# Main maxima row and pattern maxima as four products in four row groups of TensorE

## What is computed

```python
qf = jnp.concatenate([q_nope, q_pe], -1)
kf = jnp.concatenate([k_nope, k_pe], -1)
scores = jnp.einsum('bhqd,bhkd->bhqk', qf, kf) * scale
probs = jax.nn.softmax(scores.astype(jnp.float32), axis=-1).astype(dt)
ctx = jnp.einsum('bhqk,bhkd->bhqd', probs, v)
main_out = ctx.transpose(0, 2, 1, 3).reshape(b, s, H * D_V) @ o_w.T

p_scores = jnp.einsum('bhqd,bhkd->bhqk', pq, pk) * PD ** (-0.5)
p_probs = jax.nn.softmax(p_scores.astype(jnp.float32), axis=-1).astype(dt)
p_ctx = jnp.einsum('bhqk,bhkd->bhqd', p_probs, pv)
pattern_out = p_ctx.transpose(0, 2, 1, 3).reshape(b, s, HID) @ sp_o_w.T
gates = jax.nn.softmax(hidden_states @ gate_w.T + gate_b, axis=-1)
return gates[..., 0:1] * main_out + gates[..., 1:2] * pattern_out
```

## Time and profile before

| | us |
|---|---|
| median of three runs | 800.05 (797.66 to 802.2) |
| profiled execution | 798.77 |
| its span, first to last instruction | 797.0 |

### The profile page before, as it was taken

One profiled execution on the slowest core, in us unless ns is written; L12 is line 12 of the kernel. 1 busy time (PEld: TensorE's weight loads), 2 busy tenths in 40 slices (PEclk: granted clock), 3 DMA queues, 4 the chain that ended last, 5 costly groups with the idle time before them and its releaser, 6 DMA issues. The chain is left out here.

```text
span 797.0 us, 13842 instructions
## 1 busy us (share of the span) xinstructions
PE 754.4 (95%) x5456; PEld 475.2 (60%) x5456; DVE 582.2 (73%) x673; ACT 392.9 (49%) x500; POOL 433.7 (54%) x277
## 2 busy tenths in 40 slices
PE   5888989999999999999999999999999999989995
PEld 5865655555656565656655556565656654438874
DVE  6857756766779677957776779677857799997647
ACT  4443445555555555554555555555555554542352
POOL 1243039554955495549545944594478446282433
PEclk9989999999999999999999999999999999999998
DMA  9796571016201630163026102620252413331001
GB/s 237 280 246 245 121 145 28 1 56 120 68 1 38 124 95 1 38 130 115 2 76 125 54 1 61 114 81 1 71 89 79 137 42 97 110 100 35 1 1 53
DMA packets 97796, 68.13 MB, mean 85 GB/s; under 512 B 66434, under 2 KB 76228, under 8 KB 97476
## 3 DMA queue, kind: packets, MB, share of 16 engines
q1 hardware_dynamic: 97732, 67.25, 33.3%
HBM read 41.23 MB, written 17.04 MB: 73 GB/s over the span
## 5 line engine op out<-in xcount | busy, mean ns | idle before, releaser
L1011 POOL TENSOR_TENSOR acc<-acc,em 128x1024 f32<-128x1024 f32 x96 | 237.2, 2471 | 55.1 <-ACT em L1068 52.2
L1148 DVE TENSOR_REDUCE m2p<-xb 128x2 f32<-128x1024 f32 x128 | 156.1, 1222 | 74.1 <-PE xb L1313 73.9
L1156 DVE TENSOR_REDUCE m<-xb 128x2 f32<-128x1024 f32 x128 | 155.9, 1218 | 53.9 <-PE xb L1313 53.8
L1059 ACT ACTIVATE ep<-xb 128x1024 f32<-128x1024 f32 x128 | 131.3, 1025 | 115.9 <-PE xb L1313 115.9
L1068 ACT ACTIVATE em<-xb 128x1024 f32<-128x1024 f32 x128 | 131.1, 1024 | 92.6 <-PE xb L1313 88.3
L1349 PE MATMUL pvm<-em,cpair 128*32 128x512 f32 x1024 | 136.7, 606 | 0.0
L974 POOL TENSOR_TENSOR rot<-rot,sin 128x512 f32<-128x512 f32 x32 | 41.2, 1287 | 126.7 <-DMA rot<-raw 126.7
L1313 PEld LDWEIGHTS xb<-pq,pk 49*128 49x128 f32 x256 | 23.9, 184 | 107.1 <-issue 99.5
L1011 POOL TENSOR_TENSOR acc<-em 128x1024 f32<-128x1024 f32 x16 | 38.2, 2387 | 76.1 <-PE xb L1462 67.1
L1360 PE MATMUL pvp<-ep,vp 128*32 128x512 f32 x512 | 66.7, 592 | 0.0
L1313 PE MATMUL xb<-pk,pq 48*128 48x512 f32 x256 | 56.6, 440 | 9.2 <-ACT ep L1059 4.7
(11 more groups left out here) (277 smaller groups left out, 1301.5 us busy)
## 6 DMA issues: line engine op xcount, KB each, us to landing
rot<-raw SPq DMA_DIRECT2D x128, 64.0 KB, 2.4
pk<-spqk_d SPq DMA_DIRECT2D x48, 128.0 KB, 4.2
sums<-rec_d SPq DMA_DIRECT2D x32, 128.0 KB, 2.8
ctx_d<-ctxr SPq DMA_DIRECT2D x14, 256.0 KB, 2.1
pq<-spqk_d SPq DMA_DIRECT2D x48, 64.0 KB, 2.3
wraw<-wst_d SPq DMA_DIRECT2D x7, 384.0 KB, 5.8
em<-in_o_w SPq DMA_DIRECT2D x1, 2048.0 KB, 7.6
vp<-vp_d SPq DMA_DIRECT2D x8, 256.0 KB, 4.5
```

Of the source, the lines that this page charges most:

```text
L1011: pool.tensor_tensor(acc[:, :, :], before, em[:, j:j + 2, :], ALU.add).then_inc(added, 1)
L1059: act.activation(ep[:, j:j + 2, :], src[:, :, :], ACT.Exp, scale=PAT_SCALE).then_inc(ep_ready, 1)
L1148: dve.tensor_reduce(m2p[:, 2 * tp:2 * tp + 2, t, kt], src[:, :, :], AX, ALU.max).then_inc(x_dve, 1)
L1156: dve.tensor_reduce(m2[:, q, :, t, kt], src[:, :, :], AX, ALU.max).then_inc(x_dve, 1)
```

## The change

In slots 1 to 7 (`quad_at`), in the steps that have pattern maxima, the step's main maxima `mm` come before `M`, and the first `pm` comes behind `M`. `M` leaves out its seventh pair; in its place, `quad` issues four products: `sel` with `mr` on 32 rows (0 to 31 and 64 to 95), which closes `M`, and the pattern maxima on 16 rows (32 to 47 and 96 to 111). A second `pm` of a step is one pair of 16 rows. The 16 rows are the third slot of the stacks, which now holds the high part of both queries and keys, so these maxima come from high x high alone. `load_stacks` only swaps which slot holds which part; its number of DMAs stays. Slot 0 keeps the 48-row products. `PM_STEP` becomes 1, 1, 1, 1, 2, 2, 1, 2, 1, 2, 1, 1 in steps 2 to 13, sixteen as before, so twelve quads a slot and 84 in all.

```diff
-PM_STEP = [0, 0, 1, 2, 1, 2, 1, 2, 1, 2, 1, 2, 1, 0, 0, 0]
+PM_STEP = [0, 0, 1, 1, 1, 1, 2, 2, 1, 2, 1, 2, 1, 1, 0, 0]
...
+def quad_at(v, s):
+    return 1 <= v < NP and PM_STEP[s] > 0
...
         if v <= NP:
             step.append(("T", s))
-        if v < NP:
-            step += [("pm", pm + i) for i in range(min(PM_STEP[s], 1))]
+        maxima = []
+        if v <= NP and s + MM_LATE < 16:
+            maxima.append(("mm", MM_LATE + s))
+        if v < NP and s >= 16 - MM_LATE:
+            maxima.append(("mm", s - (16 - MM_LATE)))
+        if quad_at(v, s):
+            step += maxima
         if v <= NP:
             step.append(("M", s))
-        if v < NP:
-            step += [("pm", pm + i) for i in range(1, PM_STEP[s])]
+        if quad_at(v, s):
+            step += [("pm", pm + i) for i in range(PM_STEP[s])]
             pm += PM_STEP[s]
-        if v <= NP and s + MM_LATE < 16:
-            step.append(("mm", MM_LATE + s))
-        if v < NP and s >= 16 - MM_LATE:
-            step.append(("mm", s - (16 - MM_LATE)))
+        else:
+            step += maxima
...
-                            lo = int(slot == (2 if w == 0 else 1))
+                            lo = int(slot == (0 if w else 1))
...
-                return paired(out, [(xkh, xqh), (xkh, xql), (xkl, xqh), (ykh, yqh), (ykh, yql), (ykl, yqh),
-                                    (sel[:, :], mr[:, queries])], 64)
+                pairs = [(xkh, xqh), (xkh, xql), (xkl, xqh), (ykh, yqh), (ykh, yql), (ykl, yqh)]
+                if quad_at(it + 1, s):
+                    return paired(out, pairs, 64, False)
+                return paired(out, pairs + [(sel[:, :], mr[:, queries])], 64)
+
+            def quad(v, s, i, out):
+                main, queries = x_bank(v, ("M", s)), half_of(s // NT)
+                for h in range(2):
+                    at = slice(64 * h, 64 * h + 32)
+                    mm = pe.matmul(main[:, h, :], sel[at, :], mr[at, queries], start=False, stop=True)
+                mm.then_inc(x_ready, 1)
+                return pattern_maxima(v, i, out)
+
+            def pattern_maxima(v, i, out):
+                b, t, tp, kt = v % 2, i // 4, i // 2 % 2, i % 2
+                for h in range(2):
+                    at = slice(64 * h + 2 * PD, 64 * h + 3 * PD)
+                    mm = pe.matmul(out[:, h, :], pq[at, b, tp, t::4], pk[at, b, tp, half_of(kt)], start=True, stop=True)
+                return mm
```

More of the change, by code:

```diff
@@ L1306, in passes, with paired @@
                 return mm
-            def paired(out, pairs, rows):
+            def paired(out, pairs, rows, closed=True):
                 for n, (w, x) in enumerate(pairs):
@@ L1312, in paired @@
                         at = slice(64 * h, 64 * h + rows)
-                        mm = pe.matmul(out[:, h, :], w[at, :], x[at, :], start=(n == 0), stop=(n == len(pairs) - 1))
+                        mm = pe.matmul(out[:, h, :], w[at, :], x[at, :], start=(n == 0),
+                                       stop=(closed and n == len(pairs) - 1))
                 return mm
@@ L1362, in pattern_values, with x_tile @@
                 mm.then_inc(pvp_done, 1)
-            def x_tile(v, tile):
+            def x_tile(v, s, tile):
                 kind, i = tile
@@ L1376, in x_tile @@
                     mm = main_scores(v - 1, i, out)
+                    if quad_at(v, s):
+                        return
                 elif kind == "P":
@@ L1409, in x_tile @@
                     t, tp, kt = i // 4, i // 2 % 2, i % 2
-                    mm = paired(out, [(pq[:, b, tp, t::4], pk[:, b, tp, half_of(kt)])], 3 * PD)
+                    if v == 0:
+                        mm = paired(out, [(pq[:, b, tp, t::4], pk[:, b, tp, half_of(kt)])], 3 * PD)
+                    elif x_tiles[n - 1][1][0] == "M":
+                        mm = quad(v, s, i, out)
+                    else:
+                        mm = pattern_maxima(v, i, out)
                 elif kind == "mm":
@@ L1467, in tensor_program @@
                     for tile in xs[v][s]:
-                        x_tile(v, tile)
+                        x_tile(v, s, tile)
                     if s == 0 and v >= 2:
```

## The result

The kernel after takes 804.71 us (median of 12 runs, 801.82 to 806.76) against 799.62 us for the kernel before beside it (12 runs, 796.91 to 802.2): a ratio of 1.0071 [1.0055, 1.0087], slower by 5.1 us. The profiled execution took 803.35 us, 801.6 of them span, 4.6 more than before.

A forecast was written before the change was run, and what follows sets the result against it. TensorE was taken as the bound from step 6 to the next slot's step 1; steps 2 to 5 gain 0.71 us, later steps lose 2.23, +10.4 us over seven slots, giving 810 us, range 787 to 818.

The forecast's parts named there:

- the sum: Over slots 1 to 7: +1.52 us in each of six slots and +1.27 in slot 7, +10.4 us.
- What bounds the kernel: TensorE's work is on the path from step 6 to the next slot's step 1; steps 3 to 5 have waits.
- The price of the quad: Each quad costs 0.09 + 0.46 = 0.55 us against 0.47 for the pairs removed: +0.08 where TensorE is the path.
- Rival (a): In each quad, 32-row groups mix with 64-row products for free, 0.31 us cheaper: 790 us; chance 0.22.
- Rival (b): The quad's four products don't run side by side or their loads queue, 0.23 us more: 829 us; chance 0.12 with smaller form.
- Rival (c): The switch is paid, but the quad's strided loads cost no more than plain ones, 0.42 us: 799 us; chance 0.10.
- The wait after steps 4, 8 and 12: The next step's `mm` waits for the buffer of `M`, still read by its exponential: 0.09 us lost each.
- Steps 6 and 7: Three VectorE reductions in each make TensorE wait 0.53 and 0.44 us; the steps take 4.59 and 5.35 us.
- Rival (d): The waits of steps 6 and 7 don't come: 7 us less, 803 us; counted in the first case, together 0.56.
- the 0.57 us of step 5: In step 5 the projection no longer waits for the exponential of `M`, as `mm` is three tiles back: 0.57 us gained.

The follow-up runs named there:

- with pairs: Kernel after with all products in 64-row groups, pairs in place of quads, its order and plan kept: 800.42 us, ratio to before 1.0029.
- The order alone: Kernel after with pairs in place of quads and the plan of the kernel before, new order kept: 798.04 us, ratio to before 0.9986.
- the plan alone: Kernel before with one line changed, the second `pm` of step 5 moved to step 13: 793.16 us, ratio to before 0.9946.
- plain-weight run: Kernel after with pattern maxima weights from 128 neighbouring queries instead of every fourth, only the time read: 797.37 us, ratio to before 0.9992.
- best version: Kernel after with pairs in place of quads and the second `pm` of step 6 moved to step 3: 792.35 us, ratio to before 0.9916.

## Why the prediction came out as it did

The forecast was 810 us and the sign was right; the measured loss of 5.1 us is half of the 10.4 of the sum.

- **What bounds the kernel:** right. TensorE is busy through steps 6 to 15 but for 0.06 us, all in step 6, and each added part of a microsecond shows there. The end of the rotary chain did not move with TensorE's order (9.6 us from the first rotary product to the wait for `rc` in both), so what steps 2 and 3 saved was lost there, as said. The part up to step 6 gained 0.75 where the sum had 0.71.
- **The price of the quad:** right. 0.32 and 0.56 us against 0.33 and 0.55, and +0.07 a step in steps 8, 10, 11 and 12 against +0.08. Rival (a) falls: a change from 64 to 32 rows is paid like any other. Rival (b) falls: all four start within 0.01 us. Rival (c) falls: only with plain weights does its number come (0.43 against 0.42). The strided load of 16 rows takes 0.31 us like that of 48. The Trainium skill (TensorEngine Tiling (Array Packing), Key Properties) has the drain at a change of mode, and these rows agree, with 0.09 us for it.
- **The wait after steps 4, 8 and 12:** wrong in size. I took 0.67 us from the quad's start until `M` is complete, a time from a strided `pm` pair, for both halves of the quad. `M`'s own two products have plain weights: its exponential starts after 0.54 us (398.11 to 398.65) and only the reduction of `pm` after 0.67. The exponential ends at 399.67, as `T` of the next step begins, and `mm`, a pair later, doesn't wait. The 0.09 in steps 9 and 13 didn't come, and step 5 is 0.06 below its forecast.
- **Steps 6 and 7:** the mechanism is right, the sizes somewhat large. Slot 4 after:

```profile
367.96 1.61 DVE L1184 TENSOR_TENSOR ctxr<-ctxr,sums 128x512 f32<-128x512 f32 x1
369.50 1.21 DVE L1164 TENSOR_REDUCE m<-xb 128x2 f32<-128x1024 f32 x1
370.08 0.49 PE L1349 MATMUL xb<-mr,sel 32*128 32x512 f32 x2
370.77 0.31 PEld L1358 LDWEIGHTS xb<-pk,pq 16*128 16x128 f32 x2 [0.38 <-DVE m L1164]
...
373.24 0.18 PEld L1321 LDWEIGHTS xb<-qxh,kxh 64*128 64x128 f32 x2 [0.27 <-DVE m2p L1156]
```

  VectorE's division ends at 369.57 here. The reduction of `mm` follows it at once and frees its buffer at 370.71, and the second `pm` goes in step 6; `M` of step 7 waits for that one's reduction. The run with the second `pm` in step 10 gives both steps without the waits: 3.83, and a pair of 0.24 more for the second `pm`, is 4.07 for step 6, and 4.92 for step 7. So the waits cost 0.44 and 0.24 where the forecast had 0.53 and 0.44, and the steps are 4.51 and 5.16 instead of 4.59 and 5.35. Rival (d), no waits at all, falls.
- **The sum:** in steps 6 to 15 1.77 a slot where I had 2.23; the waits of steps 6 and 7 are 0.28 of the difference and those of steps 9 and 13 0.17. With the first part, slots 1 to 6 lose 5.8 us in the two parts and slot 7 0.7 as a whole: 6.5 against the forecast 10.4. The span lost only 4.6, since 2.0 were won outside these parts: in slots 1 to 6 the rotary product began 2.2 us earlier in all after the slot's start (sum of six: 91.6 before, 89.5 after), slot 1 began 1.6 earlier, and the stretch behind slot 7 took 1.8 longer. The first varies from slot to slot and from kernel to kernel with the arrival of DMAs; no experiment here moved a DMA, so whether the change shifts it is open. The other two go with the granted clock in parts that the change leaves alone: it is 0.77 before and 0.89 after from 45 to 60 us, 0.86 and 1.00 from 85 us to slot 1, and 1.00 and 0.87 in 13 us at the end of slot 8 (from 712.0 and from 714.8 us). There a wait for `acc`, which GpSimd writes, is also 0.87 us longer (2.92 against 2.05), for which I have no cause. My sum had no term for them, so the 4.6 us between these two executions are in part luck.

What I didn't see ahead of the chip is that the plan was the larger part. By the two parts, moving one `pm` from step 6 to step 3 gives 1.15 us a slot with pairs (44.10 to 42.95), while the quads cost 0.76. The forecast had both losses, but credited the new order with the 0.57 us of step 5 in which the projection no longer waits. The order alone leaves step 5 at 8.02 and the plan alone brings it to 6.89, so that term belongs to the plan.

## What to carry to other kernels

With three buffers in turn, ask of each tile which one used its buffer before, and how late that is read: one added tile in a step shifts every tile behind it by a buffer, and that decided between 0 and 2 us a step here, more than the products themselves. Packing small products side by side saved one pair here (0.24 us), but they had another shape than their neighbours: the leaving (0.09 us) and the load that is no longer hidden (0.10 plain, 0.23 strided) took most of that with plain weights and more than all of it with strided ones. And a product that closes one tile shouldn't stand behind a wait that belongs to another tile.

## What the runs showed of the hardware

- A product of 32 rows after one of 64, with the same 128 columns, pays the change of shape (0.32 us to the next start instead of 0.23), and a product of 32 and one of 16 rows (in four row groups) stand side by side without a price between them.
- Four products of 512 columns in four row groups take the time of one pair (0.24 us, an estimate: 0.43 in the plain-weight run, less 0.09 and 0.10).
- TensorE's granted clock fell after single waits of 1.39 us (with quads and the `pm` in step 13) and of 2.98 us (slot 1 of the best version), though TensorE had been busy for the whole of the 33 us up to the step of the first of them. The stretches have 0.83 and 0.72 of the full clock. Waits of 1.38 and 1.39 us in other slots and with pairs, and of 1.67 us in slot 1 of the kernel before, brought no fall. So a wait of this length can cost more than itself: 1.6 us more in steps 6 to 15 where the clock fell (47.2 against 45.55).
